# Second norm on the vector engine, a hand-written order for the first block, and eight landing places for weights

## The chip, the cores and the metric

One core of a Trainium2 chip runs the whole program. The metric is the device time in microseconds (us) of one execution. The engines are called by the profile's short names: PE (matrix engine, with its weight loads as PEld), DVE (vector engine), ACT (scalar engine), POOL (general engine) and SP (issues DMAs).

## What is computed

Two layers over x of shape 2 x 4096 x 256, all float32. First `x + layernorm(attention(layernorm(x)))`, then the same with a mixture of eight experts:

```
# attention: 8 heads of 32, chunks of 64, a running state per head
inter  = qq @ state
scores = (qq @ kk.T) * tril
o      = inter + scores @ vv
state += kk.T @ vv
o = rmsnorm(o / denom) ; out = o @ Wo.T
# experts: every one of the 8 is computed for every row, then weighted
gate, up = x @ Wg, x @ Wu
out = sum_e weights[e] * ((silu(gate) * up) @ Wd)
```

## The kernel before

The 4096 rows of both sequences are cut into 16 blocks of 256 rows (so 512 tokens, four tiles of 128). Each float32 matrix product is made of three products of rounded parts: a high part (written by ACT as a copy, `*_hi`) and the rest (a subtraction on DVE, `*_lo`).

The program is a pipeline over blocks. While the experts of block i-1 run, the attention of block i is slipped in between them, step by step. The table `STEPS` has 28 slots and says which attention steps come in which slot. In `rest`, expert e and half m own two slots. On DVE the order there is:

```
hidden(e, m, f)                      # h = silu(gate) * up
attention(4 * e - 4 + 2 * m, a)      # even slot
add_down(e - 1, m, f)                # sum of experts so far
low_hidden(e, m, f)                  # h_lo, which PE's down(e, ..) waits for
attention(4 * e - 3 + 2 * m, a)      # odd slot
```

PE goes through `up(e, m)`, even slot, `down(e - 1, m)`, odd slot. `down(e, 0)` waits until `low_hidden(e, 1)` is done (`h_lo_ready` of 2e+2), so it uses what expert e left during the `up` before it. Every engine works its own list strictly in order; semaphores are the only link.

The attention steps at the end of a block are: `wo` (output product), its copy to `rows` on ACT, `ln2_stats` (mean and variance on DVE, inverse root on POOL), `ln2_apply` (scale and shift on ACT), `ln2_add` (residual sum into x1 on DVE), `ln3_stats`, `ln3_apply` (ACT), and `ft` (transposes on PE for the experts), whose result is copied by `ft_out`. Most steps exist for half 0 and half 1 of a block.

Block 0 has no experts to hide behind. Its order is `FIRST_STEPS`, the same list for all engines, and between its steps ACT and DVE split the 24 weight units of 256 KB (`high_of_unit`, `low_of_unit`). These land by DMA in six places of the tile `late`; a place is loaded again when its unit has been split. `warm` sends dummy matmuls to PE.

Of the kernel before, what the change touches and what calls it, by code (L numbers as in the profile page):

```python
# [21 lines left out]
P = 128  # L22
# [63 lines left out]
FIRST_STEPS = [  # L86
    [("xt", 0), ("xt", 1)],
    [("kv", 0), ("q", 0)],
    [("q", 1), ("kt", 0)],
    [("su", 0), ("s", 0)],  # L90
    [("kv", 1)],
    [("o", 0), ("kt", 1)],
    [("su", 1)],
    [("s", 1), ("norm_stats", 0)],
    [],
    [("o", 1), ("norm_apply", 0)],
    [("ot", 0), ("norm_stats", 1)],
    [("wo", 0)],
    [("norm_apply", 1), ("carry",), ("ln2_stats", 0)],
    [("ot", 1)],  # L100
    [("ln2_apply", 0)],
    [("wo", 1), ("ln2_add", 0), ("ln3_stats", 0)],
    [("ln2_stats", 1)],
    [("ln3_apply", 0), ("ln2_apply", 1)],
    [("ft", 0), ("ln2_add", 1), ("ln3_stats", 1)],
    [("ft_out", 0)],
    [("ln3_apply", 1)],
    [("ft", 1)],
    [("ft_out", 1)],
    [],  # L110
]

FIRST_WARM = {("kv", 0): 4, ("s", 0): 1, ("kv", 1): 2, ("s", 1): 3, ("o", 1): 4, ("ot", 0): 4, ("wo", 0): 5, ("ot", 1): 5,
              ("wo", 1): 4, ("ft", 0): 10, ("ft", 1): 14}
# [8 lines left out]
PSUM_STEPS, FIRST_PSUM_STEPS = psum_steps(STEPS), psum_steps(FIRST_STEPS)  # L123
# [3 lines left out]
def build_program(nc, x, wq_t, wkv_t, wo_t, norm_w, wg, wu, wd, wr, temperature, out):  # L127
# [4 lines left out]
    with ctx:  # L132
# [34 lines left out]
        ot_hi, ot_lo = (xt[:, 0, :].rearrange("p (b n) -> p b n", b=B) for xt in (xt_hi, xt_lo))  # L167
# [10 lines left out]
        NSTAGE = 6  # L178
        late = sb("late", [P, NSTAGE * 512])
# [9 lines left out]
        shift1, shift2, shift3, shift4 = (sb(f"shift{n}", [P, TILES]) for n in (1, 2, 3, 4))  # L189
# [6 lines left out]
        minus_half, minus_one = sb("minus_half", [P, 2, H]), sb("minus_one", [P, TILES])  # L196
        euler = sb("euler", [P, TILES, E])
# [45 lines left out]
        wo_copied = counter("wo_copied", 2)  # L243
        x1_ready = counter("x1_ready", 2)
        ln2_applied = counter("ln2_applied", 2)
# [5 lines left out]
        moments_ready = [counter(f"moments{n}_ready", k) for n, k in ((1, 1), (2, 2), (3, 2), (4, 2))]  # L251
        rstd_ready = [counter(f"rstd{n}_ready", k) for n, k in ((1, 1), (2, 2), (3, 2), (4, 2))]
# [19 lines left out]
        stage_loaded = [sem(f"stage_loaded{n}") for n in range(NSTAGE)]  # L272
# [44 lines left out]
        def att_half(step, a):  # L317
            n = number_of(step, a) % 2
            columns = {"q": 512, "kv": 512, "s": 512, "su": B * HG * PAIR, "o": B * HPG * VA}.get(step[0], 256)
            return att_ps[:, 2 * n, :] if step[0] == "q" else att_ps[:, 2 * n:2 * n + 2, 0:columns]  # L320


        def prob_of(p, a):
            return probs[0 if psum_order(a) is FIRST_PSUM_STEPS else p]
# [23 lines left out]
        def stage(u):  # L348
            n = (u + 4) % NSTAGE
            return n, late[:, 512 * n:512 * n + 512].rearrange("p (k n) -> p k n", k=2)  # L350
# [26 lines left out]
        def _(sp):  # L377
# [9 lines left out]

            sp.sem_inc(out_stored[0], out_stored[2])
            load_x(0)
            sp.dma_start(wq_raw, wq_t.rearrange("(k p) n -> p k n", p=P)).then_inc(att_w_loaded[0], 16)  # L390
            sp.dma_start(wkv_raw, wkv_t.rearrange("(k p) n -> p k n", p=P)).then_inc(att_w_loaded[1], 16)
# [22 lines left out]
        def _(pe):  # L414
# [47 lines left out]
            def att_step(step, a):  # L462
# [10 lines left out]
                if kind == "xt":  # L473
                    k = step[1]
                    for t in range(TILES):
                        if psum_order(a) is FIRST_PSUM_STEPS:
                            pe.wait_ge(xn_ready[0], t + 1)
                        elif t == 0:
                            reach(pe, xn_ready, a, TILES)
                        last = nc.tensor.transpose(dst[:, t // 2, t % 2 * P:t % 2 * P + P], rows[:, t, k * P:k * P + P],  # L480
                                                   ident[:, :])
                elif kind == "q":
                    g = step[1]
                    reach(pe, xt_ready, a, KT)
                    last = products(dst, [((wq_hi[:, k, g * P:g * P + P], wq_lo[:, k, g * P:g * P + P]),
                                           (xt_hi[:, k, :], xt_lo[:, k, :])) for k in range(KT)])
                elif kind == "kv":
                    p = step[1]
                    reach(pe, xt_ready, a, KT)
# [11 lines left out]
                elif kind == "s":  # L501
                    p = step[1]
                    reach(pe, q_ready, a, HG)
# [12 lines left out]
                elif kind == "o":  # L516
# [6 lines left out]
                    if psum_order(a) is FIRST_PSUM_STEPS:  # L523
# [28 lines left out]
                elif kind == "wo":  # L552
                    p = step[1]
                    reach(pe, ot_ready, a, p + 1)
                    for b in range(B):
                        last = products(dst[:, b, :],
                                        [((ot_hi[:, b, g * P:g * P + P], ot_lo[:, b, g * P:g * P + P]),
                                          (wo_hi[:, g, :], wo_lo[:, g, :])) for g in range(HG)])
# [80 lines left out]
            for n, steps in enumerate(FIRST_STEPS):  # L639
                for step in steps:  # L640
                    warm(FIRST_WARM.get(step, 0))
                    if step == ("kv", 0):
                        pe.wait_ge(w_ready, 2)
                    if step == ("wo", 0):
                        pe.wait_ge(w_ready, ATT_W)
                    att_step(step, (0, 0))
            warm(2)
# [6 lines left out]
            att_step(ROUTER_T, (0, 0))  # L654
            pe.wait_ge(w_ready, ATT_W + UNITS)
            first_expert((1, 0), (0, 0))
# [18 lines left out]
        def _(act):  # L675
# [11 lines left out]
            def normalise_x(a):  # L687
                for t in range(TILES):
                    ln_apply(1, 1, a, rows, xs, [t], shift1, rstd1).then_inc(xn_ready[0], 1)
# [4 lines left out]
            def att_step(step, a):  # L694
                kind = step[0]
                if step in PSUM_STEPS and kind not in ("s", "su", "ft"):
                    reach(act, att_done, a, number_of(step, a) + 1)
                    src = att_half(step, a)
                if kind == "xt":
                    copy(halves(xt_hi[:, step[1], :]), src).then_inc(xt_hi_ready[0], 1)  # L700
                elif kind == "q":
                    copy(q_t[:, step[1], :], src).then_inc(q_ready[0], 1)
# [9 lines left out]
                elif kind == "o":  # L712
                    p = step[1]
                    reach(act, on_ready, a, p - 1)
                    for i in range(2):
# [6 lines left out]
                elif kind == "ot":  # L722
                    copy(ot_hi, src).then_inc(ot_hi_ready[0], 1)
# [10 lines left out]
                elif kind == "ln2_apply":  # L734
                    p = step[1]
                    ln_apply(2, p + 1, a, rows, rows, range(2 * p, 2 * p + 2), shift2, rstd2).then_inc(ln2_applied[0], 1)
# [41 lines left out]
            def high_of_unit(u):  # L778
                n, raw = stage(u)
                act.wait_ge(stage_loaded[n], 16 * ((u // NSTAGE) + 1))  # L780
                copy(w_hi[:, u, :, :], raw).then_inc(w_hi_ready, 1)
# [39 lines left out]
            act.wait_ge(att_w_loaded[0], 16)  # L821
            copy(wq_hi[:, :, :], wq_raw).then_inc(w_hi_ready, 1)
            normalise_x((0, 0))
            act.wait_ge(att_w_loaded[1], 16)
            copy(wkv_hi[:, :, :], wkv_raw).then_inc(w_hi_ready, 1)
            for step in FIRST_STEPS[0]:
                att_step(step, (0, 0))
            act.wait_ge(wo_scaled, 1)
            copy(wo_hi[:, :, :], wo_raw).then_inc(w_hi_ready, 1)
            for n, steps in enumerate(FIRST_STEPS):  # L830
                if n > 0:
                    for step in steps:
                        att_step(step, (0, 0))
                high_of_unit(n)
            act.wait_ge(temp_ready, 1)
            act.wait_ge(w_ready, ATT_W + UNITS - 2)
# [6 lines left out]
            high(0, 1, (0, 0))  # L843
            first_expert((1, 0), (0, 0), None)
# [19 lines left out]
        def _(dve):  # L864
# [8 lines left out]
            def ln_stats(n, src, tiles, bn, mv):  # L873
# [6 lines left out]
                last.then_inc(moments_ready[n - 1][0], 1)  # L880

            def x_stats(a):
                reach(dve, x_loaded, a, 32)
                ln_stats(1, xs, range(TILES), bn1, mv1)

            def att_step(step, a):
                kind = step[0]
                if kind == "xt":
                    k = step[1]
                    reach(dve, xt_hi_ready, a, k + 1)  # L890
                    low(halves(xt_lo[:, k, :]), att_half(step, a), halves(xt_hi[:, k, :])).then_inc(xt_ready[0], 1)
# [376 lines left out]
```

## Time and profile before

| what | value |
|---|---|
| median of 3 runs | 1507.53 us (1507.41 to 1508.8) |
| profiled execution: own time, span | 1508.8 us, 1507.1 us |
| PE busy over the span | 1468.6 us (97%) |
| DVE, ACT, POOL busy | 997.0 us (66%), 680.4 us (45%), 453.7 us (30%) |
| first expert matmul of block 0 starts | 69.55 us |
| PE busy in 0 to 80 us | 56.75 us |
| PE busy in 266 to 359 us | 92.63 us of 93 |

The span runs from the first to the last instruction of the profiled execution. The mean granted clock of PE over it is 0.994 of full speed.

### The profile page before, as it was taken

To read this page: it belongs to the slowest core of one execution; us is meant where nothing else is said; L and a number is where in the kernel's file an instruction comes from. 1 tells how busy PE (TensorE), PEld (TensorE's weight loads), DVE (VectorE), ACT (ScalarE), POOL (GpSimd) and SP (SyncE) were. 2 spreads that over 40 slices of the span, in tenths; PEclk is the share of its full clock that TensorE was granted. 3 is DMA by queue.
4 is the path that set the end of the run, shared out by engine and by line. 5 is a ranking of instruction groups with operands and counts; after the bars stand their busy time and mean duration, and the time that the engine had idled before them with its cause. 6 is when DMAs were issued, how large, how long until landed. Compare 5 with 4: busy or idle time off the path is not lost. (4 is left out here: it accounts for less than half of the span.)

```text
span 1507.1 us, 37448 instructions
## 1 busy us (share of the span) xinstructions
PE 1468.6 (97%) x14436; PEld 1280.9 (85%) x14436; DVE 997.0 (66%) x2388; ACT 680.4 (45%) x1261; POOL 453.7 (30%) x720
## 2 busy tenths in 40 slices
PE   7799999999999999999999999999999999999997
PEld 6678888888888888888888888888888888888886
DVE  4646766666676766766666676766766666776765
ACT  4543544445344453545445344453535445344433
POOL 1422512234141332512234141332513234141231
PEclk9999999999999999999999999999999999999999
DMA  3300000000000000000000000000000000000000
GB/s 113 112 1 2 21 7 14 14 14 14 0 14 14 14 14 0 21 7 14 14 14 14 0 14 14 14 14 0 25 3 14 14 14 14 0 14 16 2 8 22
DMA packets 25345, 24.59 MB, mean 16 GB/s; under 512 B 2016, under 2 KB 25056, under 8 KB 25312
## 3 DMA queue, kind: packets, MB, share of 16 engines
q1 hardware_dynamic: 25312, 24.13, 5.0%
q8 instruction: 23, 0.38, 0.1%
q14 instruction: 10, 0.08, 0.0%
HBM read 15.74 MB, written 8.39 MB: 16 GB/s over the span
## 5 line engine op out<-in xcount | busy, mean ns | idle before, releaser
L677 ACT ACTIVATE h_hi<-late 128x512 fp32r<-128x512 f32 x256 | 161.6, 631 | 271.7 <-DVE late L956 271.5
L956 DVE TENSOR_TENSOR late<-late,up_ps 128x512 f32<-128x512 f32 x256 | 175.4, 685 | 158.0 <-PE up_ps L422 100.6
L422 PE MATMUL down_ps<-w_hi,h_hi 128*128 128x256 f32 x976 | 264.5, 293 | 0.0
L422 PE MATMUL down_ps<-w_hi,h_lo 128*128 128x256 f32 x976 | 253.9, 282 | 0.0
L758 ACT ACTIVATE late<-gate_ps 128x512 f32<-128x512 f32 x256 | 151.9, 593 | 220.9 <-PE gate_ps L422 216.3
L1164 POOL TENSOR_TENSOR rms_in<-rms_in,minus_half 128x16 f32<-128x16 f32 x32 | 93.8, 2930 | 510.7 <-DVE rms_in L920 510.7
L978 DVE SCALAR_TENSOR_TENSOR late<-down_ps,route,late 128x256 f32<-128x256 f32 x364 | 158.6, 477 | 105.6 <-PE down_ps L422 102.7
L871 DVE TENSOR_TENSOR h_lo<-late,h_hi 128x512 fp32r<-128x512 f32 x256 | 175.5, 685 | 64.7 <-ACT h_hi L677 64.7
L422 PE MATMUL gate_ps<-ft_hi,w_hi 128*128 128x512 f32 x512 | 204.3, 399 | 0.7 <-ACT ft_hi L677 0.4
L422 PE MATMUL gate_ps<-ft_hi,w_lo 128*128 128x512 f32 x512 | 203.0, 397 | 0.0
L422 PE MATMUL up_ps<-ft_hi,w_hi 128*128 128x512 f32 x512 | 199.3, 389 | 0.0
L422 PE MATMUL up_ps<-ft_hi,w_lo 128*128 128x512 f32 x512 | 199.2, 389 | 0.0
L422 PE MATMUL down_ps<-w_lo,h_hi 128*128 128x256 f32 x976 | 196.4, 283 | 0.0
L422 PEld LDWEIGHTS down_ps<-w_hi,h_hi 128*128 128x128 f32 x976 | 184.8, 189 | 10.5 <-issue 3.0
L422 PEld LDWEIGHTS down_ps<-w_hi,h_lo 128*128 128x128 f32 x976 | 185.8, 190 | 4.4
L422 PE MATMUL gate_ps<-ft_lo,w_hi 128*128 128x512 f32 x512 | 159.0, 392 | 0.0
L422 PE MATMUL up_ps<-ft_lo,w_hi 128*128 128x512 f32 x512 | 157.8, 389 | 0.0
L422 PEld LDWEIGHTS down_ps<-w_lo,h_hi 128*128 128x128 f32 x976 | 151.6, 191 | 0.0
L1134 POOL TENSOR_TENSOR shift<-mv,minus_one 128x2 f32<-128x2 f32 (+1 forms) x112 | 32.6, 291 | 372.0 <-DVE mv L879 372.0
L422 PEld LDWEIGHTS gate_ps<-ft_lo,w_hi 128*128 128x128 f32 x512 | 96.4, 188 | 21.9
L422 PEld LDWEIGHTS up_ps<-ft_hi,w_hi 128*128 128x128 f32 x512 | 96.2, 188 | 21.1
L422 PEld LDWEIGHTS up_ps<-ft_hi,w_lo 128*128 128x128 f32 x512 | 96.2, 188 | 20.0
(161 smaller groups left out, 2571.6 us busy)
## 6 DMA issues: line engine op xcount, KB each, us to landing
xs<-in_x SPq DMA_DIRECT2D x32, 256.0 KB, 2.9
out_rows<-late SPq DMA_DIRECT2D x32, 256.0 KB, 2.2
late<-in_wg SPq DMA_DIRECT2D x8, 256.0 KB, 3.3
late<-in_wu SPq DMA_DIRECT2D x8, 256.0 KB, 2.7
late<-in_wd SPq DMA_DIRECT2D x8, 256.0 KB, 3.0
late<-in_wkv_t SPq DMA_DIRECT2D x1, 512.0 KB, 5.4
late<-in_wq_t SPq DMA_DIRECT2D x1, 256.0 KB, 4.6
late<-in_wo_t SPq DMA_DIRECT2D x1, 256.0 KB, 4.7
```

What stands on the lines that cost most here:

```text
L422: last = nc.tensor.matmul(dst, lhs, rhs, start=n == 0, stop=n == len(terms + low_terms) - 1)
L677: return nc.scalar.activation(dst, src, ACT.Copy)
L758: nc.scalar.activation(h_f[:, m, :], gate_ps[:, :], ACT.Silu).then_inc(silu_ready[0], 1)
L871: return nc.vector.tensor_tensor(dst, src, high_part.bitcast(f32), ALU.subtract)
L956: nc.vector.tensor_tensor(h_f[:, m, :], h_f[:, m, :], up_ps[m][:, :], ALU.mult).then_inc(h_ready[0], 1)
L978: last = nc.vector.scalar_tensor_tensor(dst[:, t, :], src, route[:, t, e:e + 1], acc[:, t, :], ALU.mult, ALU.add)
L1134: nc.gpsimd.tensor_tensor(shift[:, tiles], mv[:, tiles, 0], minus_one[:, tiles], ALU.mult)
L1164: nc.gpsimd.tensor_tensor(rms_f[:, p, :, :], rms_in[:, p, :, :], minus_half[:, :, :], ALU.pow)\
```

## The change

Three things are changed.

1. The second norm. `ln2_apply` on ACT is gone. On DVE, `ln2_stats` now also subtracts the mean (two `tensor_scalar` instructions on 128x256), and `ln2_add` multiplies by the inverse root and adds xs in one `scalar_tensor_tensor` per tile (two instead of one addition on 128x512). POOL computes the root only. In `STEPS`, `("ln2_add", 1), ("ln3_stats", 1)` stand in slot 22 instead of 23, and both `ln3_apply` one slot earlier. This holds for all blocks.
2. Block 0. PE, ACT, DVE and POOL have lists of their own. The load of x, its norm, the transposes, q, k and v are done in row halves; the first and third norm are applied by DVE.
3. Weights land in eight places: six in `late`, two in `x1`. The experts start on six units instead of waiting for all 24 before `first_expert`.

```
     [("wo", 0), ("ot", 1)],
     [("ln2_stats", 0)],
-    [("wo", 1), ("ln2_apply", 0)],
+    [("wo", 1)],
     [("ln2_stats", 1), ("ln2_add", 0), ("ln3_stats", 0)],
-    [],
-    [("ln2_apply", 1), ("ln2_add", 1), ("ln3_stats", 1)],
+    [("ln2_add", 1), ("ln3_stats", 1)],
     [("ln3_apply", 0)],
     [("ln3_apply", 1)],
+    [],
     [("ft", 0), ("ft", 1), ("ft_out", 0), ("ft_out", 1)],
...
+FIRST_PE = [("xt", 0), ("kv", 0), ("q", 0), ("xt", 1), ("su", 0), ("kv", 1), ("kt", 0), ("kt", 1), ("s", 0), ("q", 1), ("su", 1),
+            ("o", 0), ("s", 1), ("o", 1), ("ot", 0), ("wo", 0), ("ot", 1), ("wo", 1), ("ft", 0), ("ft", 1)]
...
+FIRST_DVE = [("x_stats", 0), ("x_norm", 0), ("low", "wkv"), ("xt", 0), ("x_stats", 1), ("scale", "wo"), ("low", "wq"),
+             ("x_norm", 1), ("low", "wo"), ("xt", 1), ("unit", 0), ("su", 0), ("unit", 1), ("unit", 2), ("unit", 3), ("unit", 4),
+             ("unit", 5), ("unit", 6), ("s", 0), ("unit", 7), ("unit", 8), ("su", 1), ("unit", 9), ("norm_stats", 0), ("s", 1),
+             ("unit", 10), ("unit", 11), ("unit", 12), ("unit", 13), ("norm_apply", 0), ("norm_stats", 1), ("unit", 14),
+             ("ot", 0), ("unit", 15), ("unit", 16), ("unit", 17), ("norm_apply", 1), ("ln2_stats", 0), ("ot", 1), ("ln2_add", 0),
+             ("ln3_stats", 0), ("ln2_stats", 1), ("unit", 18), ("ln2_add", 1), ("ln3_stats", 1), ("ln3_norm", 0), ("unit", 19),
+             ("ln3_norm", 1), ("ft_out", 0), ("ft_out", 1), ("unit", 20), ("unit", 21), ("unit", 22), ("unit", 23)]
...
                     ln_stats(2, rows, range(2 * p, 2 * p + 2), bn2, mv2)
+                    reach(dve, moments_ready[1], a, p + 1)
+
+                    for t in range(2 * p, 2 * p + 2):
+                        last = nc.vector.tensor_scalar(rows[:, t, :], rows[:, t, :], mv2[:, t, 0:1], None, ALU.subtract)
+                    last.then_inc(centred[0], 1)
                 elif kind == "ln2_add":
                     p = step[1]
-                    ts = slice(2 * p, 2 * p + 2)
-                    reach(dve, ln2_applied, a, p + 1)
+                    reach(dve, rstd_ready[1], a, p + 1)
+                    reach(dve, centred, a, p + 1)
                     reach(dve, x1_copied, a, 0)
-                    nc.vector.tensor_tensor(x1[:, ts, :], rows[:, ts, :], xs[:, ts, :], ALU.add).then_inc(x1_ready[0], 1)
+                    for t in range(2 * p, 2 * p + 2):
+                        last = nc.vector.scalar_tensor_tensor(x1[:, t, :], rows[:, t, :], rstd2[:, t:t + 1], xs[:, t, :],
+                                                              ALU.mult, ALU.add)
+                    last.then_inc(x1_ready[0], 1)
```

How the order moves is shown at two places. The first is DVE in the loop, around `hidden(6, 1)` (the first row, which writes `late` from `up_ps`). Before, it reads on as follows; the `SCALAR_TENSOR_TENSOR` is `add_down(5, 1)`, `h_lo` is `low_hidden(6, 1)`, and `x<-rows,xs` is `ln2_add` of half 1.

```order
L956 TENSOR_TENSOR late<-late,up_ps 128x512
L978 SCALAR_TENSOR_TENSOR late<-down_ps,route,late 128x256 x2
L871 TENSOR_TENSOR h_lo<-late,h_hi 128x512
L941 TENSOR_TENSOR x<-rows,xs 128x512
L876 BN_STATS bn<-x 128x6 x2
L879 BN_AGGR mv<-bn 128x2 x2
```

In the changed kernel the same place reads:

```order
L1002 TENSOR_TENSOR late<-late,up_ps 128x512
L985 SCALAR_TENSOR_TENSOR x<-rows,rstd,xs 128x256 x2
L904 BN_STATS bn<-x 128x6 x2
L907 BN_AGGR mv<-bn 128x2 x2
L1024 SCALAR_TENSOR_TENSOR late<-down_ps,route,late 128x256 x2
L899 TENSOR_TENSOR h_lo<-late,h_hi 128x512
```

The residual sum and the third norm's statistics of half 1 moved from behind `h_lo` to ahead of `add_down` and `h_lo`.

The second is the start of PE's list. Before, behind the fourteen dummy matmuls (`ident`), it transposes all four tiles and then needs both weights:

```order
L460 MATMUL gate_ps<-ident 128x128 x14
L480 MATMUL att_ps<-ident,rows 128x128 x8
L460 MATMUL gate_ps<-ident 128x128 x4
L422 MATMUL att_ps<-wkv_hi,xt_hi 128x512
L422 MATMUL att_ps<-wkv_hi,xt_lo 128x512
```

In the changed kernel it reads:

```order
L474 MATMUL gate_ps<-ident 128x128 x14
L493 MATMUL att_ps<-ident,rows 128x128 x4
L474 MATMUL gate_ps<-ident 128x128 x6
L436 MATMUL att_ps<-wkv_hi,xt_hi 128x512
L436 MATMUL att_ps<-wkv_hi,xt_lo 128x512
```

Four transposes (row half 0) instead of eight stand ahead of the first product of k and v, and six dummy matmuls instead of four.

## Rows read from the trace of the kernel before

**Rows 1.** The page's busy times: busy us, share of the span, instructions.

```profile
PE 1468.6 (97%) x14436; PEld 1280.9 (85%) x14436; DVE 997.0 (66%) x2388; ACT 680.4 (45%) x1261; POOL 453.7 (30%) x720
```

**Rows 2.** PE's waits in 80 to 1480 us: total us, times, longest.

```profile
PE att_ps L564 <- ACT rows L683: 5.4, 15, 0.4
```

**Rows 3.** Timeline of PE, 326 to 342 us: start, duration, engine, what.

```profile
327.67 0.40 PE L422 MATMUL down_ps<-w_lo,h_hi 128*128 128x256 f32 x2
...
332.09 0.40 PE L422 MATMUL gate_ps<-ft_hi,w_hi 128*128 128x512 f32 x1
...
334.84 0.28 PE L422 MATMUL down_ps<-w_hi,h_hi 128*128 128x256 f32 x1
...
339.99 0.63 PE L564 MATMUL att_ps<-ident,rows 128*128 128x128 f32 x4 [0.37 <-ACT rows L683]
```

**Rows 4.** Timeline of DVE, 316 to 342 us.

```profile
328.11 0.87 DVE L978 SCALAR_TENSOR_TENSOR late<-down_ps,route,late 128x256 f32<-128x256 f32 x2 [2.08 <-PE down_ps L422]
328.90 0.68 DVE L871 TENSOR_TENSOR h_lo<-late,h_hi 128x512 fp32r<-128x512 f32 x1
329.50 0.75 DVE L876 BATCH_NORM_STATS2 bn<-rows 128x6 f32<-128x256 f32 x2
...
330.57 0.66 DVE L941 TENSOR_TENSOR x<-rows,xs 128x512 f32<-128x512 f32 x1
...
332.38 0.69 DVE L956 TENSOR_TENSOR late<-late,up_ps 128x512 f32<-128x512 f32 x1
332.98 0.87 DVE L978 SCALAR_TENSOR_TENSOR late<-down_ps,route,late 128x256 f32<-128x256 f32 x2
333.77 0.69 DVE L871 TENSOR_TENSOR h_lo<-late,h_hi 128x512 fp32r<-128x512 f32 x1
334.75 0.69 DVE L941 TENSOR_TENSOR x<-rows,xs 128x512 f32<-128x512 f32 x1 [0.29 <-ACT rows L683]
...
336.58 0.69 DVE L956 TENSOR_TENSOR late<-late,up_ps 128x512 f32<-128x512 f32 x1
```

**Rows 5.** Timeline of DVE, 0 to 110 us: `scale_first`.

```profile
94.12 0.62 DVE L966 TENSOR_SCALAR late<-late,route 128x256 f32<-128x256 f32 x2
```

**Rows 6.** Timeline of POOL, 316 to 342 us: the root of half 0's third norm.

```profile
333.26 0.72 POOL L1136 TENSOR_TENSOR rstd<-var,minus_half 128x2 f32<-128x2 f32 x1 [0.18 <-POOLq L1129]
```

**Rows 7.** Timeline of PE, 0 to 110 us.

```profile
14.94 0.76 PE L422 MATMUL att_ps<-wkv_hi,xt_hi 128*128 128x512 f32 x1 [2.36 <-DVE xt_lo L871]
...
42.98 0.63 PE L551 MATMUL att_ps<-ident,shared 128*128 128x128 f32 x4 [1.87 <-DVE shared L925]
...
50.60 0.63 PE L551 MATMUL att_ps<-ident,shared 128*128 128x128 f32 x4 [2.71 <-DVE shared L925]
...
60.51 1.09 PE L564 MATMUL att_ps<-ident,rows 128*128 128x128 f32 x4 [3.77 <-ACT rows L683]
...
69.55 0.47 PE L422 MATMUL gate_ps<-ft_hi,w_hi 128*128 128x512 f32 x1 [0.44 <-ACT ft_hi L677]
...
79.03 1.41 PE L480 MATMUL att_ps<-ident,rows 128*128 128x128 f32 x8 [2.43 <-ACT rows L683]
80.10 0.78 PE L422 MATMUL gate_ps<-ft_hi,w_hi 128*128 128x512 f32 x1
...
82.80 0.50 PE L422 MATMUL up_ps<-ft_hi,w_hi 128*128 128x512 f32 x1
```

**Rows 8.** Windows of PE: stretch, length, busy (records), granted clock, DMA share, GB/s.

```profile
80.00:82.80 2.80, 2.80 (x9) 0.50 0.00 0
...
50.00:52.00 2.00, 1.40 (x12) 1.00 0.00 0
```

**Rows 9.** Timeline of DVE, 0 to 110 us: state update `su`, then the masking of `s`.

```profile
23.81 2.53 DVE L911 TENSOR_TENSOR state<-state,att_ps 32x132 f32<-32x132 f32 x8 [7.39 <-PE att_ps L542]
26.37 1.22 DVE L895 TENSOR_TENSOR rows<-att_ps,causal 128x1024 f32<-128x1024 f32 x1
```

**Rows 10.** Timeline of POOL, 0 to 110 us: the root of the attention's norm.

```profile
38.82 3.29 POOL L1164 TENSOR_TENSOR rms_in<-rms_in,minus_half 128x16 f32<-128x16 f32 x1 [30.06 <-DVE rms_in L920]
```

More of the change, by code:

```diff
@@ L84 @@
 ]
[L86 to L111, printed above, removed]
@@ L115 @@
+FIRST_POOL = [("x_stats", 0), ("x_stats", 1), ("norm_stats", 0), ("norm_stats", 1), ("carry", 0), ("ln2_stats", 0), ("ln2_stats", 1),
+              ("ln3_stats", 0), ("ln3_stats", 1)]
+FIRST_WARM = {("kv", 0): 6, ("s", 1): 2, ("o", 1): 5, ("ot", 0): 5, ("wo", 0): 6, ("ot", 1): 3, ("wo", 1): 6, ("ft", 0): 20}
 ROUTER, ROUTER_T = ("r",), ("rt",)
@@ L271, in build_program @@
         small_loaded = sem("small_loaded")
-        stage_loaded = [sem(f"stage_loaded{n}") for n in range(NSTAGE)]
+        x_first = [sem(f"x_first{p}") for p in range(2)]
+        stage_loaded = [sem(f"stage_loaded{n}") for n in range(8)]
         w_hi_ready = sem("w_hi_ready")
@@ L319, in att_half, with is_first @@
             columns = {"q": 512, "kv": 512, "s": 512, "su": B * HG * PAIR, "o": B * HPG * VA}.get(step[0], 256)
[L320 removed]
+            if step[0] == "q" and not is_first(a):
+                return att_ps[:, 2 * n, :]
+            return att_ps[:, 2 * n:2 * n + 2, 0:256 if is_first(a) and step[0] == "q" else columns]
+        def is_first(a):
+            return psum_order(a) is FIRST_PSUM_STEPS
         def prob_of(p, a):
[L324 removed]
+            return probs[1 - p if is_first(a) else p]
         def is_last(f):
@@ L346, in unit_src, with unit_raw, unit_loads, stage_free @@
             return (wg, wu, wd)[u % 3][u // 3, :, :].rearrange("(k p) n -> p k n", p=P)
-        def stage(u):
-            n = (u + 4) % NSTAGE
-            return n, late[:, 512 * n:512 * n + 512].rearrange("p (k n) -> p k n", k=2)
+        STAGES = [4, 5, 6, 7, 1, 2, 0, 3] * 2 + [4, 5, 0, 1, 2, 3, 4, 5]
+        def unit_raw(u):
+            n = STAGES[u]
+            flat = late[:, 512 * n:512 * n + 512] if n < 6 else x1[:, 2 * n - 12:2 * n - 10, :].rearrange("p t n -> p (t n)")
+            return flat.rearrange("p (k n) -> p k n", k=2)
+        def unit_loads(u):
+            return 16 * STAGES[:u + 1].count(STAGES[u])
+        def stage_free(u):
+            earlier = [v for v in range(u) if STAGES[v] == STAGES[u]]
+            return ATT_W + earlier[-1] + 1 if earlier else {1: 1, 2: 1, 0: 2, 3: 3}.get(STAGES[u], 0)
         wq_raw = late[:, 0:512].rearrange("p (k n) -> p k n", k=KT)
@@ L638, in _ @@
             warm(14)
[L639 to L647, printed above, removed]
+            for step in FIRST_PE:
+                warm(FIRST_WARM.get(step, 0))
+                if step == ("kv", 0):
+                    pe.wait_ge(w_ready, 1)
+                if step == ("q", 0):
+                    pe.wait_ge(w_ready, 2)
+                if step == ("wo", 0):
+                    pe.wait_ge(w_ready, ATT_W)
+                att_step(step, (0, 0))
             pe.wait_ge(w_ready, ATT_W + 3)
@@ L722, in att_step @@
                 elif kind == "ot":
-                    copy(ot_hi, src).then_inc(ot_hi_ready[0], 1)
+                    copy(ot_hi[step[1]], src).then_inc(ot_hi_ready[0], 1)
                 elif kind == "wo":
@@ L819, in rest @@
                 high(0, 1, a)
[L821 to L834, printed above, removed]
+            for step in FIRST_ACT:
+                if step == ("high", "wkv"):
+                    act.wait_ge(att_w_loaded[1], 16)
+                    copy(wkv_hi[:, :, :], wkv_raw).then_inc(w_hi_ready, 1)
+                elif step == ("high", "wq"):
+                    act.wait_ge(att_w_loaded[0], 16)
+                    copy(wq_hi[:, :, :], wq_raw).then_inc(w_hi_ready, 1)
+                elif step == ("high", "wo"):
+                    act.wait_ge(wo_scaled, 1)
+                    copy(wo_hi[:, :, :], wo_raw).then_inc(w_hi_ready, 1)
+                elif step[0] == "unit":
+                    high_of_unit(step[1])
+                else:
+                    att_step(step, (0, 0))
             act.wait_ge(temp_ready, 1)
-            act.wait_ge(w_ready, ATT_W + UNITS - 2)
+            act.wait_ge(w_ready, ATT_W + 20)
             silu(0, 0, (0, 0))
@@ L889, in att_step @@
                     k = step[1]
+                    half = slice(2 * P * k, 2 * P * k + 2 * P)
+                    lo, hi = (xt[:, :, half] if is_first(a) else halves(xt[:, k, :]) for xt in (xt_lo, xt_hi))
                     reach(dve, xt_hi_ready, a, k + 1)
-                    low(halves(xt_lo[:, k, :]), att_half(step, a), halves(xt_hi[:, k, :])).then_inc(xt_ready[0], 1)
+                    low(lo, att_half(step, a), hi).then_inc(xt_ready[0], 1)
                 elif kind == "s":
```

206 lines of the change are left out of this document (123 added, 83 removed).

## The prediction

> **What bounds the kernel now.** I read the page's busy times first: PE is busy for 1468.6 us of 1507.1 [rows 1], so most of a block can only get longer, not shorter. Then PE's waits in 80 to 1480 us, the blocks in the loop: nearly all is one wait of 0.4 us per block, fifteen times, 5.4 us in sum, for ACT's third norm ahead of `ft` [rows 2]. That is all that the loop can give back. The other losses stand ahead of 80 us: the first block, in which PE waits for chains through DVE, ACT and POOL. The reader is to see there five gaps of PE of 1.87 to 3.77 us [rows 7] and that the first expert product starts only at 69.55 us and the second block's transposes at 79.03.
>
> So two questions decide: how much earlier does the first block end, and does the loop still run without a wait. The second is asked fifteen times, so a microsecond there weighs as fifteen in the first block.
>
> **The loop, step by step.** I follow one block from PE's `down(5, 0)`, whose last matmuls start at 327.67 [rows 3]. PE needs no one until `down(6, 0)` at 334.84 [rows 3]. For that, `low_hidden(6, 1)` must be done; DVE does it from 333.77, for 0.69 us, so to 334.46 [rows 4]. The slack is 0.38 us.
>
> Before that DVE works without a pause from 328.11: `add_down`, `h_lo`, then from 329.50 `ln2_stats` of half 1, `ln2_add` and `ln3_stats` of half 0, and `hidden(6, 1)` at 332.38 [rows 4]. Its input from PE is complete long before (`up(6, 1)` ends twelve matmuls, 2.75 us by the same twelve at 332.09 to 334.84, after 327.9, so near 330.7 [rows 3]): DVE is late, not PE. Whatever is put on DVE here delays `h_lo` one for one. Three things are put there:
>
> - Subtracting the mean, two `tensor_scalar` of 128x256. The same form costs 0.62 us a pair [rows 5]; with overlap of the next some 0.55, and a wait on DVE's own `moments2_ready` of some 0.15. I take 0.7 us.
> - `ln2_add` of half 0 as two `scalar_tensor_tensor` instead of one addition. No row has that form with all inputs in SBUF. The nearest has one input in PSUM and takes 0.79 us from start to start of the next (332.98 to 333.77), the addition 0.69 (330.57 to 334.75's form, 0.66 to 0.69 long) [rows 4]. Two `tensor_scalar` at 0.62 are the lower end [rows 5]. I take the nearer row, +0.1, and 0.1 to 0.15 for the waits on `centred` and `rstd2_ready`: +0.25 in all. Together `hidden(6, 1)` starts 0.95 to 1.1 us later, near 333.4.
> - `ln2_add` and `ln3_stats` of half 1 now stand between `hidden(6, 1)` and `add_down`, `h_lo`. Before, from the start of `ln2_add` at 334.75 to the next `hidden` at 336.58 they took 1.83 us [rows 4]; with the new form about 1.95.
>
> The sum: `h_lo` ends at 334.46 + 1.0 + 1.95 = 337.4, and PE, which wanted to start at 334.84, waits 2.6 to 2.7 us with the signal's delay. Behind that `down` stand PE's `up(7, 1)`, `ft`, and everything after, so the wait is paid in full. It gives back the 0.4 us of [rows 2]: `ft` needs the third norm, which now starts earlier against a PE that comes later. Net +2.3 us a block; fifteen blocks make **+34.5 us**. Bounds: 2.0 (`scalar_tensor_tensor` at 0.62 a pair, `tensor_scalar` overlapped, no extra waits) to 2.7, so +30 to +40.
>
> What ACT saves (two pairs of applies per block) buys nothing: ACT is busy 45% [rows 1], and of its instructions only the third norm's is waited for.
>
> **The clock.** A new gap of 2.7 us per block also puts PE's clock at risk. Of the five gaps, the ones of 2.36, 3.77 and 2.43 us were followed by matmuls at half the pace (0.78 us for a first 128x512 instead of 0.40), those of 1.87 and 2.71 were not [rows 3, 7]; the granted clock is 0.50 in 80.0 to 82.8 us and 1.00 in 50 to 52 [rows 8], which are the levels of 1.2 and 2.4 GHz. So a gap of this size falls sometimes. One fall costs about 1.35 us in six matmuls (80.10 to 82.80 is 2.70 [rows 7]; twelve at full speed take 2.75 [rows 3], six half of it) and a little in the transposes ahead: 1.5 us. Nothing here says how often, so I take half the blocks, 7.5 x 1.5 = **+11 us**, bounds 0 and 15 x 1.6 = +24. The Trainium skill (TensorE: Matmul & The Clock Gate, "HAM oscillation") warns only of idle stretches longer than this one; by it the term would be nothing and the forecast 11 us lower, while the rows show falls after shorter gaps.
>
> **The port.** A second rule speaks against the change. The inputs of both new `scalar_tensor_tensor` lie in SBUF. The Trainium skill (SBUF — State Buffer, "SBUF: two separate sides") says that DVE with two SBUF inputs and GpSimd lock each other out for a whole instruction; by it POOL's root of half 1 could hold `ln2_add` of half 0 for up to its length, 0.7 us or 11 us in all. But the row shows POOL's root running from 333.26 to 333.98 [rows 6] and DVE's `h_lo`, with both inputs in SBUF, starting inside it at 333.77 at its usual 0.69 us [rows 4]. I add nothing.
>
> **The first block.** Four stretches, each against before:
>
> - To the first product of k and v: 14.94 before, behind a wait of 2.36 us [rows 7]. Now PE needs one half of x, split in about 0.6 us on ACT and 0.6 on DVE behind four transposes; the dummy matmuls end where they did. I get 11.5 us, and with the short gap no half pace in it: 5 us earlier at the end of this product.
> - To the root of half 0 (38.82 before [rows 10]). DVE is now the bound from about 17.8 us: ten weight subtractions at 0.6 (start to start of a 128x512 subtraction [rows 4]), two state updates at 2.53, a mask at 1.2 [rows 9], statistics about 1: 13.3 us, so 31.1. 7.6 us earlier.
> - To `ot(1)` (50.60 before [rows 7]): mask 1.2, `o(1)` 2, copy and square 1.3, statistics 1, root 3.3 [rows 10], apply 1.1: 41.3. 9 us earlier.
> - To the first expert product (69.55 before [rows 7]). Two applies on ACT with their waits for POOL, the 3.77 us gap and the half pace behind it go away; two subtractions of the mean come in. The chain of transposes, copies, statistics, two short roots and `ft` adds up to 12.6 us: 54. With 0.1 us for each of a dozen signals, 55.
>
> Gain: **-14.5 us**, bounds -12 (signals of 0.3) and -17. The second block's transposes keep their distance of 9.5 us to it (69.55 to 79.03 [rows 7]): that chain (the last weight subtractions, statistics of x, root, apply) is the same. The eight landing places are worth nothing by themselves where, as here, DVE is behind the loads. From there all blocks are the loop's.
>
> **Sum.** Against the profiled execution's span: 1507.1 + 34.5 + 11 - 14.5 = 1538; the 1.7 us between span and own time (1508.8) stay. The median of the runs lies 1.3 under that own time, at 1507.5: 1507.5 + 31 = **1538.5 us**.
>
> **The rivals.**
> - The clock never falls in the new gaps: 1507.5 + 34.5 - 14.5 = 1527.5. For it: the gap of 2.71 us that did not fall. Against: two shorter ones that did.
> - It falls in nearly every block: 1507.5 + 34.5 + 22 - 14.5 = 1549.5. For it: three of five. Against: the loop around a gap is dense, unlike the first block.
> - On the other side: DVE's new order costs PE nothing, and the first block's gain stands alone with `ft`'s wait: 1507.5 - 14.5 - 5.4 = 1487.6. The mechanism would be that `h_lo` of (6, 1) has cover that I can't see. It decides when the new wait is under 14.5 / 15 = 0.97 us a block net of the 0.4 given back. Against: 0.38 us of slack in rows 3 and 4 with 2.9 us of work put ahead. If only half of the work counted, 1503 to 1518.
> - The first block gains nothing, since ACT's and DVE's own lists wait for each other and for the reloaded places: 1507.5 + 34.5 + 11 = 1553. Against: each list follows the order in which its inputs come.
>
> **How the numbers follow.** Chances: forecast with falls in part of the blocks (1532 to 1545) 0.40; no falls (1520 to 1532) 0.22; falls in most (1545 to 1560) 0.15; no gain in the first block 0.06; no cost in the loop 0.11, half of it 0.06. Half of that last 0.06 lies on either side of no change. Given the wait, the range is 1520 to 1560, 0.77 and part of the other cases; 1517 to 1560 holds eight in ten. A measurement here tells about 0.2% (3 us) from no change. Faster 0.13, same 0.02, slower 0.85.
>
> **What would show it.** In the changed kernel's trace: a PE wait for DVE's `h_lo` of 2.5 to 2.8 us once a block, fifteen times, ahead of `down_ps`; no wait for ACT at `ft`; half pace behind some of these gaps; the first 128x512 into `gate_ps` near 55 us and the second block's transposes near 64.5. The forecast is wrong if that PE wait is missing or under 1 us, or if the first block ends later than 60 us.

## The result and the profile after

| | before | changed |
|---|---|---|
| median | 1507.47 us (4 runs, 1507.39 to 1508.8) | 1543.13 us (4 runs, 1537.69 to 1544.67) |
| ratio | | 1.0228, 95% interval 1.0201 to 1.0254: slower |
| profiled execution: own time, span | 1508.8, 1507.1 us | 1544.2, 1542.5 us |
| mean granted clock | 0.994 | 0.986 |

The page's busy times of the changed kernel answer to [rows 1]. ACT lost 34 us of work and DVE gained 30. PE has two instructions more, but is busy 11 us longer:

```profile
PE 1479.5 (96%) x14438; PEld 1289.1 (84%) x14438; DVE 1027.0 (67%) x2492; ACT 646.1 (42%) x1189; POOL 437.5 (28%) x653
```

PE's waits in 75 to 1500 us (us in total, times, longest) answer to [rows 2]. The wait for ACT ahead of `ft` is gone; in its place stands one for DVE, six times as long:

```profile
PE down_ps L436 <- DVE h_lo L899: 36.3, 15, 2.4
```

Where it comes from is read from DVE's timeline, 322 to 334 us. It is the same expert as in [rows 4], in the block that the changed kernel works on at that time:

```profile
324.10 0.74 DVE L904 BATCH_NORM_STATS2 bn<-rows 128x6 f32<-128x256 f32 x2
...
325.28 0.65 DVE L977 TENSOR_SCALAR rows<-rows,mv 128x256 f32<-128x256 f32 x2
325.85 0.87 DVE L985 SCALAR_TENSOR_TENSOR x<-rows,rstd,xs 128x256 f32<-128x256 f32 x2
...
327.87 0.69 DVE L1002 TENSOR_TENSOR late<-late,up_ps 128x512 f32<-128x512 f32 x1
328.48 0.88 DVE L985 SCALAR_TENSOR_TENSOR x<-rows,rstd,xs 128x256 f32<-128x256 f32 x2
...
330.46 0.84 DVE L1024 SCALAR_TENSOR_TENSOR late<-down_ps,route,late 128x256 f32<-128x256 f32 x2
331.22 0.68 DVE L899 TENSOR_TENSOR h_lo<-late,h_hi 128x512 fp32r<-128x512 f32 x1
```

From `ln2_stats` at 324.10 to `hidden(6, 1)` at 327.87 are 3.77 us, where [rows 4] have 2.88 (329.50 to 332.38). Between `hidden(6, 1)` and `add_down` now lie 1.98 us of `ln2_add` and `ln3_stats` of half 1 (328.48 to 330.46). The only idle times in the stretch are 0.15 us ahead of each `BN_AGGR` (L907), as in the kernel before: DVE works through, and `h_lo` ends at 331.90. PE's timeline, 328 to 337 us, shows who stood waiting, and that `ft` (the last row, `L591`) starts without the wait that it had in [rows 3]; the wait in square brackets is the idle time ahead of the row, and what ended it:

```profile
328.98 0.61 PE L436 MATMUL up_ps<-ft_lo,w_hi 128*128 128x512 f32 x2
332.03 0.38 PE L436 MATMUL down_ps<-w_hi,h_hi 128*128 128x256 f32 x1 [2.44 <-DVE h_lo L899]
...
333.56 0.40 PE L436 MATMUL gate_ps<-ft_hi,w_hi 128*128 128x512 f32 x1
...
336.31 0.93 PE L591 MATMUL att_ps<-ident,rows 128*128 128x128 f32 x7
```

The distance from one of these fifteen waits to the next is a block's period. It is 92.43 us in five of the fourteen distances, against 90.30 before; the other nine are 93.58 to 94.02. The rows behind two of the gaps show why. First the one at 701.76, in the same view:

```profile
701.76 0.38 PE L436 MATMUL down_ps<-w_hi,h_hi 128*128 128x256 f32 x1 [2.43 <-DVE h_lo L899]
...
703.05 0.54 PE L436 MATMUL down_ps<-w_lo,h_hi 128*128 128x256 f32 x2
703.39 0.63 PE L436 MATMUL gate_ps<-ft_hi,w_hi 128*128 128x512 f32 x1
```

Then the next block's, at 795.76:

```profile
795.76 0.58 PE L436 MATMUL down_ps<-w_hi,h_hi 128*128 128x256 f32 x1 [2.43 <-DVE h_lo L899]
796.14 0.41 PE L436 MATMUL down_ps<-w_hi,h_lo 128*128 128x256 f32 x1
...
798.49 0.51 PE L436 MATMUL gate_ps<-ft_hi,w_hi 128*128 128x512 f32 x1
798.83 0.40 PE L436 MATMUL gate_ps<-ft_hi,w_lo 128*128 128x512 f32 x1
```

After the same gap the matmuls run at full pace at 332.03; at 701.76 the pace drops 1.3 us later (0.63 for a 128x512 at 703.39, not 0.40); at 795.76 it is slow at once (0.41 for a 128x256, not 0.28) and back at 798.83. The windows of PE (stretch, length, busy, granted clock, DMA share, GB/s) agree:

```profile
332.00:336.00 4.00, 3.97 (x23) 1.00 0.13 46
702.00:705.00 3.00, 3.00 (x16) 0.69 0.06 22
796.00:799.00 3.00, 3.00 (x14) 0.55 0.05 17
```

So the clock falls from 2.4 to 1.2 GHz behind ten of the fifteen gaps (145, 702 and each one after it). The fourteen periods show nine of them: the late kind adds 1.57 us, the immediate kind 1.30, together 12.9 us over 14 x 92.43.

In the first block the gain is real. PE's timeline, 10 to 75 us, answers to [rows 7]:

```profile
12.38 0.47 PE L436 MATMUL att_ps<-wkv_hi,xt_hi 128*128 128x512 f32 x1 [0.17 <-DVE xt_lo L899]
...
44.19 0.63 PE L578 MATMUL att_ps<-ident,shared 128*128 128x128 f32 x4 [0.96 <-DVE shared L963]
...
55.02 0.63 PE L591 MATMUL att_ps<-ident,rows 128*128 128x128 f32 x4 [1.45 <-DVE rows L918]
...
56.95 0.63 PE L591 MATMUL att_ps<-ident,rows 128*128 128x128 f32 x4 [1.30 <-DVE rows L918]
...
58.35 0.77 PE L436 MATMUL gate_ps<-ft_hi,w_hi 128*128 128x512 f32 x1 [0.78 <-ACT ft_hi L705]
...
69.33 1.06 PE L499 MATMUL att_ps<-ident,rows 128*128 128x128 f32 x8 [2.43 <-ACT rows L711]
```

The first expert product starts 11.2 us earlier (69.55 before), the second block's transposes 9.7 us earlier. The first expert product now meets the slow clock (0.77, then 0.63 a piece, granted 0.50 in 58 to 61), where before the product behind the transposes of 79.03 did (80.10 in [rows 7]). That is why the second block's transposes gain 1.5 us less than the first expert product, and why most of it is back behind them. By the first `down(6, 0)` of the loop the kernel is 11.1 us ahead: its gap ends at 145.57, less 2.44 of wait that is 143.13, and before `down(6, 0)` stood at 334.84 - 2 x 90.30 = 154.24.

The sum, from one profiled execution of each kernel: -11.1, then 2.44 for the first wait, 14 x (92.43 - 90.30) = 29.8, 12.9 for the nine long periods, which makes 34.0. The difference of the spans is 35.4; the other 1.4 us fit the tenth fall, behind the last of the fifteen gaps. How many falls there are differs between executions: the mean granted clock of the four is 0.986, 0.988, 0.987 and 0.991, and the last of them is the fastest (1537.69 us).

### The profile page after: what moved, and what is told of

It is laid out like the page before. It is cut to its first block and busy times, and to the rows that moved or that the text cites. A ratio compares the mean times of both kernels' runs of the same rounds, so it can differ in the third digit from the quotient of the medians.

```text
span 1542.5 us, 37390 instructions
## 1 busy us (share of the span) xinstructions
PE 1479.5 (96%) x14438; PEld 1289.1 (84%) x14438; DVE 1027.0 (67%) x2492; ACT 646.1 (42%) x1189; POOL 437.5 (28%) x653
## 5 line engine op out<-in xcount | busy, mean ns | idle before, releaser
L436 PE MATMUL down_ps<-w_hi,h_hi 128*128 128x256 f32 x976 | 268.8, 297 | 36.3 <-DVE h_lo L899 36.3
L436 PE MATMUL gate_ps<-ft_hi,w_hi 128*128 128x512 f32 x512 | 207.6, 406 | 1.0 <-ACT ft_hi L705 0.8
L436 PEld LDWEIGHTS up_ps<-ft_lo,w_hi 128*128 128x128 f32 x512 | 96.1, 188 | 20.0
```

The costliest lines, as they stand in the source:

```text
L436: last = nc.tensor.matmul(dst, lhs, rhs, start=n == 0, stop=n == len(terms + low_terms) - 1)
```

## The experiments

My theory: three terms that have nothing to do with each other. DVE's longer list ahead of `low_hidden(6, 1)` makes PE wait 2.4 us a block; the waits let the clock fall in part of the blocks; the first block gains about 11 us. The rivals: that the wait comes from the new form of the second norm as such, wherever it stands; that the long periods have another cause than the gap (the slower clock as a matter of the whole run, or of ACT's changed load); that the first block's gain and the loop's loss depend on each other; and, for the parts of the first block, my own claim that the eight landing places are worth nothing. The ratios are to the kernel before as it was timed beside each experiment: 1507.81 us for the place of half 1's steps, the first block alone, the filled gap and the spread order, 1508.74 for the other three. The traces are of one execution each.

**Only the place of half 1's steps.** Slots 22 and 23 of `STEPS`, otherwise the changed kernel:

```diff
-    [("ln2_add", 1), ("ln3_stats", 1)],
-    [("ln3_apply", 0)],
+    [],
+    [("ln2_add", 1), ("ln3_stats", 1), ("ln3_apply", 0)],
```

> The changed kernel, with the residual sum and third-norm statistics of half 1 put back behind h_lo (slot 23); the second norm stays on DVE. Theory (the place costs): of the 2.87 us that h_lo(6,1) is late, 1.98 are the place and 0.89 the arithmetic, against 0.38 us of slack; so PE's wait for h_lo falls from 2.43 to about 0.5 us a block, ft waits again for ACT, some 0.7 us, no clock falls; about 1508 us (1503 to 1513). Rival (the second norm's arithmetic on DVE costs, wherever it stands): the wait for h_lo stays over 1.5 us a block and the time over 1520.

Measured: 1508.15 us (11 runs, 1505.2 to 1510.07), ratio to before 1.0 (0.9991 to 1.0009). Of the loss of 35 us nothing is left. That is two terms that cancel, and not a loop as fast as before: the first block's gain is still in it, and the period is 90.90 us, 0.6 over before's, which makes 8.4 us in fourteen blocks. PE's waits in 75 to 1500 us:

```profile
PE down_ps L436 <- DVE h_lo L899: 7.2, 15, 0.5
```

The wait fell from 2.43 to 0.48 us, close to the 1.98 us of the moved pair, and the clock is at 0.997 over the profiled span. The time was met; one detail was not: the second wait of 0.7 us at `ft` did not come. Instead the weight load ahead of the next block's first products waits 0.3 us, once a block, for `ft_lo`, which DVE writes later. The 0.5 that remains is what the second norm's new form puts ahead of `hidden(6, 1)` (0.89 us) less the slack of 0.38 of the kernel before.

**The first block alone.** The changed kernel with the loop's old table, and the second norm in the loop back on ACT:

```diff
-    [("wo", 1)],
+    [("wo", 1), ("ln2_apply", 0)],
     [("ln2_stats", 1), ("ln2_add", 0), ("ln3_stats", 0)],
-    [("ln2_add", 1), ("ln3_stats", 1)],
+    [],
+    [("ln2_apply", 1), ("ln2_add", 1), ("ln3_stats", 1)],
     [("ln3_apply", 0)],
     [("ln3_apply", 1)],
-    [],
```

> First block and landing places of the changed kernel, loop of the kernel before (second norm by ACT, old slots). Theory (the first block's 11.1 us gain is its own and is kept): 1507.5 - 11.1 = 1496.4 us (1495 to 1498), ft wait of 0.4 us a block as before, no wait for h_lo. Rival (part of the gain is the early ring of x1 and DVE that the loop pays back, or the loop's new norm is part of it): 1500 or more.

Measured: 1500.15 us (5 runs, 1496.86 to 1500.39), ratio 0.9945 (0.9932 to 0.9959). The profiled execution is the fastest of the five, with a span of 1495.2 us, 11.9 under before's; the other four have spans of 1497.9 to 1498.7 and a mean granted clock of 0.995 for 0.997. By the time alone this misses my range of 1495 to 1498 and lands on the bound that I gave the rival, that the loop pays part of the gain back (1500 or more). The trace speaks against that rival: the period is 90.33 us, against 90.30, and the waits in the loop are those of before:

```profile
PE att_ps L592 <- ACT rows L712: 5.5, 15, 0.4
```

So the first block gives 7.7 us by the medians and 11.9 by the profiled executions. That the slower four have a further fall of the clock in their first blocks fits their lower mean, but they were not traced.

**The loop alone.** The first block, its table and the six places of the kernel before, with the changed loop; the edit is the first block's part of the diff taken back (its `FIRST_STEPS` again for all four engines, whole rows again at the load of x):

```diff
-FIRST_PE = [("xt", 0), ("kv", 0), ("q", 0), ("xt", 1), ("su", 0), ("kv", 1), ...
...
+FIRST_STEPS = [
+    [("xt", 0), ("xt", 1)],
+    [("kv", 0), ("q", 0)],
...
+        NSTAGE = 6
+        late = sb("late", [P, NSTAGE * 512])
```

> First block and six landing places of the kernel before, loop of the changed kernel. Theory (the loop's loss and the first block's gain are independent): the changed kernel plus the 11.1 us, 1543 + 11 = 1554 us (1547 to 1560 by the number of clock falls), PE waiting 2.43 us for h_lo fifteen times. Rival (the loss in the loop is set up by the new first block or the new landing places): under 1540.

Measured: 1553.37 us (5 runs, 1551.64 to 1555.24), ratio 1.0302 (1.0288 to 1.0316). The loop costs 45 us by itself, and the new first block takes 10.2 of it away (1553.37 - 1543.13). With the old loop it took 7.7, so gain and loss add up to within 2.5 us, and no dependence beyond that shows. PE's wait for `h_lo` is again 2.4 us fifteen times; in this trace the clock falls behind fewer gaps, with eight long periods of fourteen instead of nine.

**A filled gap.** Nine dummy matmuls in front of `down(6, 0)`, some 2.2 us, in the changed kernel. They write to a bank that `ft` overwrites; PE does nothing useful in them:

```diff
+                if n == 24:
+                    fill(9, a)
...
+            def fill(count, a):
+                reach(pe, ot_ready, a, 2)
+                for _ in range(count):
+                    nc.tensor.matmul(att_half(("ft", 0), a)[:, 0, 0:P], ident[:, :], ident[:, :], start=True, stop=True)
```

> The changed kernel with nine dummy matmuls (2.1 us) on PE just ahead of the waited down(6,0), into a bank that ft overwrites later; no work is taken away. Theory (a gap of 2.43 us costs its length and in about 9 of 15 blocks a clock fall of 1.4 us besides): the wait shrinks to about 0.3 us, period 92.4 us in every block, no granted clock under 1.0 after the first blocks, 1543 - 12.5 = 1530.5 us with less scatter between runs. Rival (the falls are not due to the gap, or the long periods are something else): 1540 or more.

Measured: 1532.0 us (5 runs, 1528.9 to 1532.58), ratio 1.0149 (1.0135 to 1.0163). PE's wait is 0.4 instead of 2.4 us, and DVE is as late as before:

```profile
PE down_ps L436 <- DVE h_lo L906: 6.2, 15, 0.4
```

The period is 92.43 us in every block; the windows around three of the gaps that had a fall show the clock at 1.00:

```profile
144.00:152.00 8.00, 7.58 (x49) 1.00 0.22 69
700.00:708.00 8.00, 7.58 (x52) 1.00 0.21 66
794.00:802.00 8.00, 7.58 (x54) 1.00 0.19 66
```

This parts the two costs in the loop: the wait itself (2.13 us net of what it gives back) stays, and the falls are worth 1543.13 - 1532.0 = 11.1 us by the medians. By the two spans it is 11.7. In the loop alone it is more, since this profiled execution had more slow clock in its first two blocks (granted 0.57 against 0.79 in 57 to 65 us, 0.79 against 1.00 in 68 to 76) and comes 2.9 us later to the first `down(6, 0)` (148.50 against 145.57): 11.7 + 2.9 = 14.6, which is ten falls at 1.3 to 1.6. Idle time of PE brings them on, not ACT's load or the run as a whole, which are the same here.

**Half 0 and half 1 spread out.** With half 1's steps in slot 23 alone, 0.5 us are left at `down(6, 0)`. Here half 0 is done a slot earlier, `ln2_stats` of half 1 stands alone, and half 1 follows behind `h_lo`:

```diff
-    [("wo", 1)],
-    [("ln2_stats", 1), ("ln2_add", 0), ("ln3_stats", 0)],
-    [("ln2_add", 1), ("ln3_stats", 1)],
-    [("ln3_apply", 0)],
+    [("wo", 1), ("ln2_add", 0), ("ln3_stats", 0)],
+    [("ln2_stats", 1)],
+    [],
+    [("ln2_add", 1), ("ln3_stats", 1), ("ln3_apply", 0)],
```

> The changed kernel with residual sum and third-norm statistics of half 0 moved to slot 20, where DVE idles some 2 us for down_ps, and those of half 1 in slot 23. Theory (DVE only has to reach h_lo(6,1) in time): hidden(6,1) starts earlier than in the kernel before, no wait for h_lo, and the 0.4 us at ft is gone too: 1507.5 - 11.1 - 6 = 1490.5 us (1489 to 1493). Rival (DVE has too much to do in this stretch however it is ordered): a wait of 0.5 us or more a block stays somewhere, 1498 or more.

Measured: 1490.48 us (4 runs, 1488.22 to 1491.7), ratio 0.9884 (0.9869 to 0.9899): faster than both kernels. DVE's timeline, 310 to 324 us; no two residual sums (`L985`) stand between the same pair of `h_lo` any more:

```profile
312.83 0.88 DVE L985 SCALAR_TENSOR_TENSOR x<-rows,rstd,xs 128x256 f32<-128x256 f32 x2
...
314.81 0.85 DVE L1024 SCALAR_TENSOR_TENSOR late<-down_ps,route,late 128x256 f32<-128x256 f32 x2
315.57 0.69 DVE L899 TENSOR_TENSOR h_lo<-late,h_hi 128x512 fp32r<-128x512 f32 x1
...
319.58 0.68 DVE L899 TENSOR_TENSOR h_lo<-late,h_hi 128x512 fp32r<-128x512 f32 x1
320.18 0.87 DVE L985 SCALAR_TENSOR_TENSOR x<-rows,rstd,xs 128x256 f32<-128x256 f32 x2
```

From the loop's entry to 1450 us PE has no wait left that comes once a block; all that its view of waits lists there are two single ones:

```profile
PE att_ps L436 <- DVE h_lo L899: 0.3, 1, 0.3
PE gate_ps L436 <- ACT late L786: 0.2, 1, 0.2
```

The period is 89.75 us. So the second norm on DVE costs PE nothing where it is spread, although DVE does as much as in the changed kernel.

**The six landing places.** The spread kernel again, but its unit weights go round six places instead of eight:

```diff
-        STAGES = [4, 5, 6, 7, 1, 2, 0, 3] * 2 + [4, 5, 0, 1, 2, 3, 4, 5]
+        STAGES = [4, 5, 1, 2, 0, 3] * 2 + [1, 2, 0, 3] + [4, 5, 0, 1, 2, 3, 4, 5]
```

> The rebalanced kernel with the six places of late alone (x1 unused for weights). Theory (DVE is behind the loads in the first block): first expert product within 0.5 us of the 57.1 us it has with eight places, time 1490 us, no change beyond the scatter. Rival (the two extra places carry the first block's gain): the first expert product 2 us or more later, 1493 or more.

Measured: 1494.76 us (5 runs, 1493.07 to 1497.05), ratio 0.9913 (0.9899 to 0.9926). That is 4.3 us more than with eight, against my expectation of none. ACT's timeline, 0 to 45 us, shows three loads that come too late, none of which makes ACT wait with eight places:

```profile
21.11 0.63 ACT L705 ACTIVATE w_hi<-late 128x512 fp32r<-128x512 f32 x1 [1.99 <-DMA late<-in_wg]
...
34.28 0.63 ACT L705 ACTIVATE w_hi<-late 128x512 fp32r<-128x512 f32 x1 [1.96 <-DMA late<-in_wu]
...
38.49 1.32 ACT L705 ACTIVATE w_hi<-late 128x512 fp32r<-128x512 f32 x2 [3.58 <-DMA late<-in_wd]
```

With eight, the only wait for a unit in that stretch is this one, and with six it comes too, at 45.65:

```profile
41.80 1.33 ACT L705 ACTIVATE w_hi<-late 128x512 fp32r<-128x512 f32 x2 [3.06 <-DMA late<-in_wg]
```

Behind these copies, in ACT's strict list, stand its copies for the attention, and PE waits for what follows from them. PE's timeline with six places:

```profile
43.58 0.55 PE L436 MATMUL att_ps<-wo_hi,xt_hi 128*128 128x256 f32 x1 [4.54 <-DVE xt_lo L899]
```

With eight the same product starts at 39.68:

```profile
39.68 0.35 PE L436 MATMUL att_ps<-wo_hi,xt_hi 128*128 128x256 f32 x1 [0.86 <-DVE xt_lo L899]
```

The first expert product is 4.35 us later (61.48 against 57.13). The start of this `wo` product differs between executions, too: with eight places it lies between 39.53 and 41.04 in six traces, so 43.58 is late against all of them, by 2.5 to 4.1 us. The matmuls behind the gap of 4.54 us are also at half pace (0.55 us for the first, then 0.42 a 128x256 instead of 0.28).

**Dummy work ahead of the first expert product.** The spread kernel with more dummies at `ft`, and three ahead of the first expert product:

```diff
-              ("wo", 1): 6, ("ft", 0): 20}
+              ("wo", 1): 6, ("ft", 0): 24, ("ft", 1): 5}
...
+            warm(3)
```

> The rebalanced kernel with dummy matmuls ahead of ft(0) (24 for 20), ft(1) (5) and the first expert product (3). Theory (the short waits of 1.45, 1.30 and 0.78 us around ft in sum let the clock fall, which costs some 1.4 us): the first 128x512 into gate_ps takes 0.47 us instead of 0.77, the second block's transposes come 1.2 to 1.6 us earlier, 1489 us. Rival (the fall only moves to the next gap of 2.4 us ahead of the second block's transposes, as in the kernel before): same time as the rebalanced kernel within 0.5 us.

Measured: 1488.04 us (4 runs, 1486.94 to 1489.18), ratio 0.9864 (0.9849 to 0.9879), the lowest median of all; its interval overlaps that of the kernel without the dummies (0.9869 to 0.9899), so the 2.4 us between the medians are likely, not certain, and the two profiled executions stand the other way (spans of 1487.5 and 1486.5). PE's timeline shows the product at full pace:

```profile
57.91 0.47 PE L436 MATMUL gate_ps<-ft_hi,w_hi 128*128 128x512 f32 x1
58.22 0.39 PE L436 MATMUL gate_ps<-ft_hi,w_lo 128*128 128x512 f32 x1
```

It starts 0.8 us later than without the dummies, but they are not the cause: the first `wo` product, ahead of all that were added, is 0.9 us later already (40.60 against 39.68). The second block's transposes come at 67.40 instead of 68.11, 0.7 us earlier and not the 1.2 to 1.6 that I expected. There the clock then falls (granted 0.76 in 65 to 70 us, against 1.00 without the dummies), so part of the gain is given back, as the rival had it. Whether anything is gained on the whole this run does not settle.

## Why the prediction was right, and where it was off

The forecast was 1538.5 us, the result 1543.13: the sign, the cause and its place were right, and the miss is 4.6 us, of 36. In part the closeness is luck. Against the two spans the wait was put 2.2 us too high (34.5, measured 32.3), the clock 3.3 too low (11, measured 14.3) and the first block's gain 3.4 too high (14.5, measured 11.1); the first error takes away a third of the other two.

- **What bounds it.** PE at 97% and a loop with no more than a `ft` wait to give back held. That wait is worth more than its 0.37 us: with it gone the period is 89.75 in place of 90.30, so 0.55 us a block.
- **DVE's chain ahead of `hidden(6, 1)`.** I put it at 0.95 to 1.1 us later, measured 0.89 (3.77 - 2.88). Its parts: the subtraction of the mean 0.57 (325.28 to 325.85) and 0.11 for the wait ahead of it (324.10 to 325.28 is 1.18, 329.50 to 330.57 in [rows 4] is 1.07), together 0.68 for my 0.7; and 0.21 for the new form of `ln2_add` (325.85 to 327.87 is 2.02, 330.57 to 332.38 is 1.81) for my 0.25. The total was right and its parts were not: from its start to the next instruction the new form takes 0.90 us, where I took 0.79 from the row with an input in PSUM, and no wait shows beside it.
- **`ln2_add` and `ln3_stats` of half 1 ahead of `add_down`.** 1.95 predicted, 1.98 measured; moving this pair alone took 1.95 of the 2.43 us of wait away.
- **The wait.** 2.6 to 2.7 predicted, 2.43 measured; net +2.3 a block predicted, +2.13 measured. The term of the sum is 32.3 us (2.44 + 29.8) instead of 34.5, within its bounds. That the wait for `ft` is given back held.
- **The clock.** I had half the blocks at 1.5 us and took 11; it was ten of fifteen gaps at 1.3 to 1.6. The filled gap measures the term at 11.1 us by the medians and the long periods at 12.9, 14.3 with the tenth fall. The kind was right and the size near, but "half the blocks" was a choice with nothing behind it, and the number of falls differs between executions. Which blocks fall I could not have said, and still cannot: the matmuls ahead of the gaps are the same in all, and so is the wait (2.43 us, only the last 2.28).
- **The port.** I added nothing, and DVE is not held: from `ln2_add` of half 1 at 328.48, with POOL's root at 328.55 inside it, to `ln3_stats` at 329.39 are 0.91 us; in the spread kernel the same instruction at 320.18, with POOL idle, takes 0.91 to the next as well. By the Trainium skill (SBUF — State Buffer, "SBUF: two separate sides") whichever of the two starts first keeps the other out for its whole instruction; this trace does not agree, since VectorE keeps its length behind a root that started first (331.18 and 331.22), and only POOL's gets longer (last section). Nothing of PE's waits for that root.
- **The first block.** -14.5 predicted with bounds of -12 and -17, -11.1 measured in the trace, 7.7 to 10.2 us by the medians: outside the bounds. This is the term that was mis-sized most. The mis-sized terms by place: the first product at 12.38 (11.5 predicted), the root of half 0 at 32.80 (31.1; row below), `ot(1)` at 44.19 (41.3), the first expert product at 58.35 (55). The lag grows at each step: the first in the k and v chain, then 0.8, then 1.2, then 0.45 us. I counted durations and too little between them. Of the 1.7 us at the root, DVE's timeline shows 0.2 for a later start (18.01 for 17.8), 0.6 for the `xt_lo` of half 1, which is not in my sum, 0.55 in two waits (for PE ahead of the mask, for ACT ahead of the statistics) and 0.2 in longer statistics. My parts up to `ot(1)` add up to 41.0 and not 41.3. Some of the lag is scatter: in five traces with this first block the first expert product starts between 56.87 and 58.36. The transposes of the second block, predicted at 64.5, came at 69.33: they did not keep their distance of 9.5 us but stand 10.98 behind the first expert product, since the expert products between them ran in part at half pace, which was not foreseen; the gap of 2.43 us ahead of them is the same as before. POOL's timeline, 25 to 60 us, with the row that answers to [rows 10]:

```profile
32.80 2.90 POOL L1225 TENSOR_TENSOR rms_in<-rms_in,minus_half 128x16 f32<-128x16 f32 x1 [18.34 <-DVE rms_in L958]
```

- **The step that failed: "The eight landing places are worth nothing by themselves where, as here, DVE is behind the loads".** With six of them 4.3 us are lost in the spread kernel; the changed kernel itself was not timed with six. I had looked at DVE, which is behind; but a unit is first copied by ACT, which is not behind the loads, and which stands waiting for a landing with the attention's copies behind it. This step didn't move the forecast, since the eight places were in it; it would have misjudged the same change with six.
- **The rivals.** "DVE's new order costs PE nothing" (1487.6) is excluded, but the mechanism it describes can be built: the spread order moves the same work to where it has cover and comes to 1490.48. "No gain in the first block" (1553) is excluded: with the old first block the time is 10.2 us longer. "No falls" (1527.5) and "falls in nearly every block" (1549.5) lie either side; ten falls in fifteen blocks are between them.

Open: why the clock falls behind some of equal gaps only, and what makes up the 1.2 us of lag between the root and `ot(1)`, of which 0.7 are missing in the spread kernel's trace (10.71 us from the root to `ot(1)`, here 11.39). Neither was tried further.

## What to carry to other kernels

Work moved to an engine that is busy 66% costs nothing or 30 us by where in its list it stands: count what lies between the other engine's input and the one result that it needs, in each block, and spread new work over several such stretches. A wait of over 2 us on the matrix engine costs more than its length, since the clock may fall behind it; matmuls in the gap, even useless ones, bring the second part back, and show how large it is. A landing place is judged from the first engine that reads it, and from what stands behind that read in its list, not from the engine that is last.

## What the runs showed of the hardware that was not expected

- POOL's root of 128x2 takes 0.72 us beside `add_down` (one input in PSUM) and the start of `h_lo` [rows 6]. In the changed kernel it takes 0.98 us beside `ln2_add` (328.48) and the statistics, and 1.29 beside `h_lo` (331.22) and `hidden`, while VectorE's instructions keep their length. That inputs of VectorE in SBUF stretch it fits these rows, but not the one at 325.70: there the root takes 0.78 us although `ln2_add` of half 0 runs beside it from 325.85. No run measured it by itself. POOL's timeline, 326 to 333 us:

```profile
325.70 0.78 POOL L1194 TENSOR_TENSOR rstd<-var,minus_half 128x2 f32<-128x2 f32 x1 [0.18 <-POOLq L1179]
...
328.55 0.98 POOL L1186 TENSOR_TENSOR rstd<-var,minus_half 128x2 f32<-128x2 f32 x1 [0.18 <-POOLq L1179]
...
331.18 1.29 POOL L1186 TENSOR_TENSOR rstd<-var,minus_half 128x2 f32<-128x2 f32 x1 [0.18 <-POOLq L1179]
```

- Behind gaps of 2.43 us each, with the same matmuls ahead, the clock fell at once, 1.3 us later or not at all. From 702 us on the first two kinds alternate block by block (0.73 and 0.55 granted in 3.6 us around and behind each gap's end), with periods of 94.0 and 93.7 us.
- A stop of PE of 0.37 us costs 0.55 us: PE has the same list in the spread kernel's loop as before and no wait once a block, and the period is 89.75 against 90.30. A stop of 2.43 us costs 2.68 (92.43 against 89.75).
- `scalar_tensor_tensor` on 128x256 with all inputs in SBUF takes 0.87 us a pair, the same as with one input in PSUM (0.87), but the next instruction, which reads what it wrote, starts 0.91 us behind it; behind `add_down` the next starts after 0.79.
